# Spreading softmax denominators over partitions: DRAM bounce and stride-zero load in place of TensorE products

## The reference

```python
x = x + _L0_xattn_ref(_layernorm(x, axis=-1), ctx_768, Wq, Wk, Wv, Wo, bo)
# in it, with heads h = 16, d = 64, scale = 64 ** -0.5:
#   q = heads(x @ Wq); k, v = heads(ctx @ Wk), heads(ctx @ Wv)
#   attn = softmax(q k^T * scale, over the 1444 keys)
#   out = merge(attn @ v) @ Wo + bo
```

## Time and profile before

| | us |
|---|---|
| three executions | 5123.05, 5123.84, 5160.94 |
| median | 5123.84 |
| span of the profiled execution | 5139.5 |
| TensorE busy in it | 4115.3 |
| VectorE | 2994.6 |
| ScalarE | 2115.7 |
| GpSimd | 1733.6 |

### The profile page before, as it was taken

One profiled execution on the slowest core, in us unless ns is written; L12 is line 12 of the kernel. 1 busy time (PEld: TensorE's weight loads), 2 busy tenths in 40 slices (PEclk: granted clock), 3 DMA queues, 4 the chain that ended last, 5 costly groups with the idle time before them and its releaser, 6 DMA issues. The chain is left out here.

```text
span 5139.5 us, 86857 instructions
## 1 busy us (share of the span) xinstructions
PE 4115.3 (80%) x26550; PEld 2846.4 (55%) x26550; DVE 2994.6 (58%) x4577; ACT 2115.7 (41%) x3227; POOL 1733.6 (34%) x1171
## 2 busy tenths in 40 slices
PE   8899999999979988778789999994763434336699
PEld 4588888888867746534445555552432222223377
DVE  4344445444523444446545676656459999996433
ACT  3255555555522232124324555542235555551122
POOL 2266666666524232004310000000225555541033
PEclk8799999999969988799867999996876666667699
DMA  2000000000002203220022222210010101000011
GB/s 85 1 10 19 10 19 19 19 10 19 10 1 62 59 1 91 48 61 2 1 56 47 65 62 62 62 33 1 1 24 18 26 17 26 17 19 1 0 61 48
DMA packets 124607, 152.80 MB, mean 30 GB/s; under 512 B 86912, under 2 KB 110224, under 8 KB 124080
## 3 DMA queue, kind: packets, MB, share of 16 engines
q1 hardware_dynamic: 124208, 147.72, 11.5%
HBM read 109.43 MB, written 2.66 MB: 22 GB/s over the span
## 5 line engine op out<-in xcount | busy, mean ns | idle before, releaser
L989 POOL TENSOR_TENSOR pexp_lo<-arena,pexp_hi 128x800 fp32r<-128x800 f32 x384 | 635.7, 1655 | 443.2 <-POOLq L988 442.5
L2173 DVE TENSOR_REDUCE arena<-ps 100x1 f32<-100x482 f32 (+1 forms) x768 | 489.9, 657 | 266.8 <-DVEq L2160 256.5
L2053 DVE TENSOR_REDUCE arena<-ps 128x1 f32<-128x482 f32 (+3 forms) x624 | 392.9, 656 | 365.6 <-DVEq L2031 354.8
L1330 ACT ACTIVATE arena<-ps 128x800 f32<-128x800 f32 x384 | 322.3, 839 | 500.3 <-ACTq L1328 497.8
L2471 DVE MATCH_REPLACE8 arena<-arena 100x1444 f32<-100x1444 f32 x256 | 420.8, 1656 | 0.0
L1420 ACT ACTIVATE arena<-ps 128x800 f32<-128x800 f32 x384 | 315.5, 837 | 249.8 <-ACTq L1419 243.6
L3202 PE MATMUL ps<-kst,qs 96*100 96x482 f32 (+1 forms) x768 | 376.2, 492 | 43.0 <-PEq L3156 39.4
L935 POOL TENSOR_TENSOR max_diag<-w_const,arena 100x800 fp32r<-100x800 f32 x160 | 246.8, 1543 | 436.5 <-POOLq L933 436.5
L3331 PE MATMUL ps<-w_const,w_cross 100*128 100x100 f32 x192 | 43.2, 380 | 374.1 <-PEq L3328 374.1
L1331 ACT ACTIVATE pexp_hi<-ps 128x800 fp32r<-128x800 f32 x384 | 319.5, 832 | 0.0
L2573 DVE TENSOR_TENSOR arena<-ps,arena 128x400 f32<-128x400 f32 x256 | 147.1, 575 | 280.2 <-DVEq L2572 280.2
(11 more groups left out here) (393 smaller groups left out, 9621.0 us busy)
## 6 DMA issues: line engine op xcount, KB each, us to landing
ctxT<-in_ctxT SPq DMA_DIRECT2D x56, 541.5 KB
kst<-mid SPq DMA_DIRECT2D x128, 180.5 KB, 3.1
ctxk<-in_ctx SPq DMA_DIRECT2D x40, 528.0 KB
chunk<-in_ff_chunks SPq DMA_DIRECT2D x77, 193.0 KB, 2.4
arena<-gate_dram SPq DMA_DIRECT2D x64, 200.0 KB, 3.8
kst<-xn SPq DMA_DIRECT2D x64, 180.5 KB, 2.9
arena<-gate_dram SPq DMA_DIRECT2D x64, 100.0 KB, 2.6
arena<-in_ctxT SPq DMA_DIRECT2D x8, 541.5 KB
```

Of the source, the lines that this page charges most:

```text
L989: own(nc.gpsimd.tensor_tensor(pexp_lo[p % 3][:, :, :], pexp[p % 3], pexp_hi[p % 3][:, :, :], ALU.subtract))
L1330: nc.scalar.activation(pexp[p % 3], of, ACT.Exp, scale=scale).then_inc(s.pexp_ready, 1)
L2053: peak = nc.vector.tensor_reduce(mparts[0:at.stop - at.start, m, c:c + 1], bank(k, z - a, at.stop - at.start), AX.X, ALU.max)
L2173: peak = nc.vector.tensor_reduce(mparts2[:, h, c:c + 1], bank(k, z - a, S), AX.X, ALU.max)
```

## The change

The inverses no longer go through `rexp`'s block diagonal and TensorE. VectorE inverts `den_rows` in step 3 as before (`inverses`); SP stores them into a DRAM tensor `den_dram` of 1600 numbers, waits for that, and loads them back with a source whose step is zero, so that each of 97 partitions of `rexp` gets all 1600. VectorE multiplies `rexp` onto `u` in four parts, in steps 8 to 11 (`divide`); ahead of the first it waits for the load. The projection stays in step 12. The tail behind the last batch keeps the old way.

```diff
-    rexp = shared([HEADS, HEADS, S])
+    rexp = shared([C + 1, HEADS, S])
...
+    den_dram = nc.dram_tensor("den_dram", (1, HEADS * S), F32).ap()
...
         if tail:
-            items += {3: [("recips", 0, 0)], 4: [("recips", 1, 0)], 5: [("spread", 0, 0)], 6: [("spread", 1, 0)],
-                      7: [("spread", 2, 0)], 11: [("spread", 3, 0)], 12: [("project", 0, 0)]}.get(p, [])
+            items += {3: [("inverses", 0, 0)], 8: [("divide", 0, 0)], 9: [("divide", 1, 0)], 10: [("divide", 2, 0)],
+                      11: [("divide", 3, 0)], 12: [("project", 0, 0)]}.get(p, [])
...
+            def spread_inverses():
+                sp.wait_ge(s.rexp_ready, 1)
+                sp.sem_inc(s.rexp_ready, -1)
+                sp.dma_start(den_dram.rearrange("o (h t) -> (o h) t", t=S), den_rows[:, :]).then_inc(s.scratch_stored, 16)
+                sp.wait_ge(s.scratch_stored, 16)
+                sp.sem_inc(s.scratch_stored, -16)
+                sp.dma_start(rexp.rearrange("p h t -> p (h t)"), den_dram.to_broadcast([C + 1, HEADS * S])).then_inc(s.den_loaded, 16)
...
                     denominators(par)
                     load_context(2 * i + 2 + par, par)
+                    spread_inverses()
             denominators(0)
+            spread_inverses()
             denominators(1)
...
+                elif kind == "inverses":
+                    invert()
+                    dve.sem_inc(s.rexp_ready, 1)
+                elif kind == "divide":
+                    if arg == 0:
+                        dve.wait_ge(s.den_loaded, 16)
+                        dve.sem_inc(s.den_loaded, -16)
+                    hs = u[1 - par][:, 4 * arg:4 * arg + 4, :]
+                    nc.vector.tensor_tensor(hs, rexp[:, 4 * arg:4 * arg + 4, :], hs, ALU.mult).then_inc(s.dve_done, 1)
                     dve.wait_ge(s.dve_done, 1)
                     dve.sem_inc(s.dve_done, -1)
+                    dve.sem_inc(s.u_ready, 1)
...
             def side(kind, arg, b, par, ahead):
-                if kind in ("recips", "rows"):
+                if kind in ("recips", "inverses", "divide", "rows"):
                     return
```

More of the change, by code:

```diff
@@ L2032, in side_bank, with invert @@
                 return 6 + (count[0] - 1) % 2
+            def invert():
+                dve.wait_ge(s.den_loaded, 16)
+                dve.sem_inc(s.den_loaded, -16)
+                dve.wait_ge(s.u_raw_ready, 1)
+                dve.sem_inc(s.u_raw_ready, -1)
+                nc.vector.reciprocal(den_rows[:, :], den_rows[:, :]).then_inc(s.dve_done, 1)
+                dve.wait_ge(s.dve_done, 1)
+                dve.sem_inc(s.dve_done, -1)
             def side(kind, arg, b, par):
@@ L2080, in side @@
                 elif kind == "recips" and arg == 0:
[L2081 to L2085, removed]
+                    invert()
+                elif kind == "inverses":
+                    invert()
+                    dve.sem_inc(s.rexp_ready, 1)
+                elif kind == "divide":
+                    if arg == 0:
+                        dve.wait_ge(s.den_loaded, 16)
+                        dve.sem_inc(s.den_loaded, -16)
+                    hs = u[1 - par][:, 4 * arg:4 * arg + 4, :]
+                    nc.vector.tensor_tensor(hs, rexp[:, 4 * arg:4 * arg + 4, :], hs, ALU.mult).then_inc(s.dve_done, 1)
                     dve.wait_ge(s.dve_done, 1)
                     dve.sem_inc(s.dve_done, -1)
+                    dve.sem_inc(s.u_ready, 1)
                 elif kind == "recips":
-                    nc.vector.tensor_tensor(rexp, den_rows[:, :].unsqueeze(1).to_broadcast([HEADS, HEADS, S]),
+                    nc.vector.tensor_tensor(rexp[0:HEADS], den_rows[:, :].unsqueeze(1).to_broadcast([HEADS, HEADS, S]),
                                             W("const", "ident")[0:HEADS, 0:HEADS].unsqueeze(2).to_broadcast([HEADS, HEADS, S]),
@@ L3044, in side @@
                     k = side_bank()
-                    ins = mm(bank(k, GT, C + 1), W("const", "ones")[0:HEADS, 0:C + 1], rexp[:, 4 * arg:4 * arg + 4, :], start=True, stop=True)
+                    ins = mm(bank(k, GT, C + 1), W("const", "ones")[0:HEADS, 0:C + 1], rexp[0:HEADS, 4 * arg:4 * arg + 4, :], start=True, stop=True)
                 else:
@@ L3103, in batch @@
                 for p in range(4 * PAIRS):
-                    items = [it for it in sides_at(p, prep, tail) if it[0] not in ("rows", "recips")]
+                    items = [it for it in sides_at(p, prep, tail) if it[0] not in ("rows", "inverses", "divide")]
                     values(p, par)
```

## The result

Four executions of the changed kernel took 5324.83 to 5391.01 us, median 5345.92; four of the kernel before 5123.05 to 5174.02, median 5142.39. The ratio is 1.041, with a 95% interval of 1.0355 to 1.0465: slower. From the first product of batch 0 to the last step of batch 15, by the starts of TensorE's products, the 16-head stage went from 1209.5 to 1385.3 us, +175.8; the other 11 lie outside, in code that the change doesn't touch, and are less than the 51 us between the executions of before. The mean batch, of batches 1 to 14, went from 75.99 to 88.11 us.

The account below looks back on a forecast made before the run. TensorE was taken to bound the kernel. Per batch 12.8 us of wait - 1.0 for a spread + 3 of clock = 14.8, times 14.5 = +214 us on a median of 5123.84: 5338 us, range 5265 to 5450.

Parts of the forecast that it names:

- The width of the load: DRAM load into rexp: 97 rows is prime, so one DMA engine carries 97 packets one behind another.
- The path: From inverse through store and load to the first division: landing at 831.6, TensorE going on 12.8 us later per batch.
- the better bound: Load time on one engine, faster bound: 23.4 us, from the best slice of the context load at 424 GB/s.
- What the spreads give: TensorE's four spread products: three saved before the wait are worth nothing, the fourth behind it 1.0 us per batch.
- The clock: TensorE behind the wait falls to the lower clock, costing 3 us per batch.
- the 1.7 and the 7.2 us of two rows: TensorE's clock losses in two earlier stretches at 0.50, at the stage's start and in the last batch.
- The sum: All tails: 14.8 us per batch, the last tail counted half, giving +214 us and a median of 5338 us.
- The rival with many engines: Load runs on many engines and is hidden: 0.8 to 2.5 us per batch gained, say 5095 us; chance 0.12.
- deciding point, two engines: Load on two engines lands at 818.2, just when VectorE comes to the first division; from there the rival decides.
- the divisions hold up GpSimd: In the hidden case SBUF-only divisions share GpSimd's port; GpSimd falls back by up to 1.8 us.
- The second rival: Load on one engine but TensorE's clock never falls: +171 us, 5295 us; chance 0.10.
- The third: Rival: one engine does not overlap packets, 0.6 us each, load 58 us, about 5790 us; chance 0.03.

Follow-up runs that it names:

- the kernel with filled waits: Changed kernel plus 60 unread 128x400 TensorE products ahead of step 10's first side product; ratio 1.0338 to the kernel before, mean batch 85.78 us.
- 112 rows: Changed kernel with the load filling 112 partitions of rexp instead of 97, of which 97 are used; ratio 0.9943 to the kernel before, mean batch 74.61 us.
- late divisions: Changed kernel, divisions moved to steps 15 to 18, projection to 19; ratio to the kernel before 0.9949 with 97 rows, 0.9911 with 112.
- 96 and one: Changed kernel with its load split into 96 rows and 1 row, the first division waiting for both; ratio 0.9990 to the kernel before, mean batch 74.53 us.

## Why the prediction was right

**The width of the load.** This was right: the load ran on one engine, as the prime row count and the packet counts of the earlier trace rows had it. The Trainium skill ("DMA: Bandwidth & Descriptors", section "Why a DMA increments its semaphore by 16 and not by 1") has the same rule, and the runs agree with it for 1, 2, 3 and 16 engines.

**The path.** The mechanism was right, the size too long. From the end of the inverse (875.28) to the first division the prediction had 30.1 us, and 27.6 came: 0.23 to the store's issue in place of 0.4; 1.41 from there to the load's issue in place of 1.9, so the store is quicker than the gather that I priced it by the earlier trace rows; 25.97 from the load's issue in place of 27.8, a packet taking 24.9 / 97 = 0.257 us rather than 0.276. The 24.9 us lie between the forecast, 26.8 out of the earlier trace rows, and the better bound, 23.4 out of the best slice in the earlier trace rows, a little nearer the bound. From the first division to TensorE's next product 1.74 us passed, 1.63 were forecast. (Added up, the prediction's terms end at 833.2 and not at 833.4, so that its 12.8 us should be 12.6.) Counted from the batch's first product, TensorE goes on at 41.49 in place of 31.29: 10.2 us later, forecast 12.8.

**What the spreads give.** This was right at both places. Steps 5 to 7 shrank from a mean of 11.05 to 9.29 us (forecast 9.4, ScalarE's limit), and this went into the wait. Behind the wait the fourth gave 1.0: the stretch from the first chunk of step 10 on is 43.53 with the clock up, 44.49 before.

**The clock.** The forecast was 3 us per batch; the runs gave 3.86 in batch 7 and 2.3 in the mean, against the kernel with filled waits. The size is right, with some luck: the 3 was a choice between the 1.7 and the 7.2 us of two rows, and no sum. Half of the time at the lower level lies in the wait itself, where it costs nothing (896.30 to 904.60 with no product).

**The sum.** Per batch 12.1 us were measured and 14.8 forecast; the last batch grew by 6.2 (74.3 to 80.5 us), and 7.4 were forecast. Over the stage it is +176 against +214: the term that was too large is the path. That the median, 5345.92, nevertheless lies next to the 5338 forecast is partly luck. The forecast started from 5123.84, the median of three executions; that of four is 18.6 higher, and the two medians are 203.5 us apart, 28 more than the stage. These 46 us hide the 38. The scatter of executions is some 50 us, and the profiled pair is 187 apart.

**The rival with many engines** was priced about right and its cost was misplaced. The prediction gave it 0.8 to 2.5 us per batch; with 112 rows 1.4 were gained, and 2.2 with late divisions. The prediction's deciding point, two engines, is where the kernel breaks even. But the prediction had the divisions hold up GpSimd. VectorE's, GpSimd's, then TensorE's timeline of batch 7 with 112 rows:

```profile
809.40 1.67 DVE L2110 TENSOR_TENSOR arena<-arena 97x400 f32<-97x400 f32 x1 [0.45 <-DVEq L2108]
...
812.56 1.86 DVE L2110 TENSOR_TENSOR arena<-arena 97x400 f32<-97x400 f32 x1
```

```profile
809.03 1.60 POOL L1000 TENSOR_TENSOR pexp_lo<-arena,pexp_hi 128x800 fp32r<-128x800 f32 x1 [0.37 <-POOLq L999]
...
812.38 1.61 POOL L1000 TENSOR_TENSOR pexp_lo<-arena,pexp_hi 128x800 fp32r<-128x800 f32 x1 [0.45 <-POOLq L999]
```

```profile
812.22 0.46 PE L3065 MATMUL ps<-ctxT_hi,qa_hi 113*128 113x480 f32 x1 [0.62 <-PEq L3038]
```

Here GpSimd had begun first, and the divisions end 0.44 and 0.43 us behind its instruction, taking three times their 0.57 us. So VectorE was late with the chunk maxima, TensorE waited 0.62 us for a side bank (L3038), and step 10 took 3.54 us in the mean in place of 2.64. It is the lock of the earlier trace rows, with VectorE as the one that waits, as in the earlier trace rows, where the prediction's sum had GpSimd wait; the Trainium skill ("SBUF — State Buffer", section "Who interferes with whom") names it, and these rows agree. In the changed kernel it hardly shows, three of four divisions taking 0.57 us, because GpSimd has run dry behind the stopped TensorE: its timeline shows it idle for 10.81 us up to 910.51.

**The second rival** (one engine, clock up) is what the kernel with filled waits shows: 5315 beside 5147, +168 where the rival had +171, but not the time of the changed kernel. **The third**, packets that don't overlap, fell: 97 packets in 24.9 us.

## What to carry to other kernels

Before work is moved from an engine to a DMA, count the DMA engines that the transfer will use: here 97 rows went over one and took 26 us from issue to use, the last packet of 96 and one ended 3.6 us after the issue, and the small packets of the queue told it in every trace of this case. A load that lands late costs only what is queued behind the wait for it, on the waiting engine and then on the bottleneck; moving the wait by seven steps was worth as much as sixteen engines. And an operation on the bounding engine is worth its full time only where that engine would not have waited anyway: the same four products were worth 4.1 us in one place and 2.7 in another.

## What was not expected of the hardware

The clock falls in the wait, not behind it: in batch 7 TensorE's last product ended at 893.05, the lower level begins at 896.3 within the wait, and it holds to 913.4, through 8.8 us with products. The changed kernel has such a stretch in each of its 15 tails, of 10.2 to 20.5 us. And the width of the load does less than its count of engines. By the shares above a packet of 6400 B takes 0.257 us with one engine at work, 0.26 with two and 0.25 with three, but 0.34 with sixteen (14.3% of 16 x 16.7 us for 112 packets). From the load's issue to the end of its last packet the traces have 25.4, 14.6, 10.1 and 3.7 us for 97, 106, 111 and 112 rows; in each the first packet starts 0.9 to 1.0 us after the issue. Why a packet is slower among sixteen engines no run here tests. Three engines, at 37 packets each, were already as good as sixteen because the way to the first division has room for them.
